# A graph layer with linear attention beside it: the attention's second half by tiles of nodes, turned for the projection two layers later

## The reference

```python
xn = layernorm(x)
# 1. four graph layers: gather the source rows, add the edge term, relu, sum at the target, two dense layers
for l in range(4):
    m = relu(h[src] + (edge_weight @ We[l] + be[l]))
    agg = segment_sum(m, dst)
    h = relu(relu(batchnorm(((1 + eps[l]) * h + agg) @ W1[l] + b1[l])) @ W2[l] + b2[l])
# 2. linear attention over the same xn, 8 heads of 64
q, k, v = fm(xn @ Wq + bq), fm(xn @ Wk + bk), xn @ Wv + bv      # fm(t) = elu(t) + 1
kv  = einsum('shd,she->hde', k, v)
z   = 1 / einsum('shd,hd->sh', q, k.sum(0))
att = einsum('shd,hde,sh->she', q, kv, z).reshape(s, 512) @ Wp + bp
x = x + h + att
# 3. a routed feed-forward block over layernorm(x), 8 experts, the best one for each node
```

## Time and profile before

| | |
|---|---|
| median of 3 runs | 1873.07 us |
| lowest and highest | 1863.77 and 1879.77 us |
| profiled execution, time | 1876.88 us |
| profiled execution, span | 1875.0 us |
| TensorE clock granted, mean | 0.934 of full |
| busy: TensorE, VectorE, ScalarE, GpSimd | 1551.8, 1280.2, 889.9, 1108.4 us |

### The profile page before, as it was taken

The page is one execution under the profiler, slowest core; times in us unless marked ns, Lnnn a source line. Parts: engine busy times, 40 slices in busy tenths (PEclk is TensorE's granted clock), DMA queues, the critical chain, the costliest instruction groups (busy, mean ns, idle before and its releaser), DMA issues.

```text
span 1875.0 us, 20514 instructions
## 1 busy us (share of the span) xinstructions
PE 1551.8 (83%) x6418; PEld 658.6 (35%) x6418; DVE 1280.2 (68%) x2344; ACT 889.9 (47%) x990; POOL 1108.4 (59%) x1073
## 2 busy tenths in 40 slices
PE   2677878766799888987899998997999989988694
PEld 2223333322343333332443333333433333334373
DVE  6678876768444999777546876876348877785533
ACT  1454443444305556665415665674146657663220
POOL 4777777777006767777016777774057777770122
PEclk8898999988999999999899998999999999998797
DMA  6767676667228867776238887874378887766244
GB/s 221 197 196 201 188 197 179 179 204 227 60 72 237 223 196 202 216 216 191 77 110 242 238 245 222 224 214 131 92 220 237 236 254 218 214 200 218 106 125 156
DMA packets 119349, 355.34 MB, mean 190 GB/s; under 512 B 19760, under 2 KB 24200, under 8 KB 118981
## 3 DMA queue, kind: packets, MB, share of 16 engines
q0 software_dynamic: 83600, 274.01, 51.6%
q1 hardware_dynamic: 35637, 79.95, 13.2%
HBM read 333.93 MB, written 19.95 MB: 189 GB/s over the span
## 4 chain that ended last, share of the span: by engine, by line
PE 46%; POOL 19%; DVE 12%; issue 9%; DMA 7%; ACT 7%; DVEq 0%; SPq 0%; POOLq 0%; ACTq 0%
PE ps L1523 42%; POOL ring L700 17%; DVE ring L876 6%; ACT ring L1350 6%; DMA ring<-x_table,idxT 4%; DMA zT<-slot_table 2%; PE ps L1588 2%; DVE xT L1086 1%; DVE aggT L1186 1%; POOL ring L743 1%; DMA mix<-in_edge_weight 1%; DVE lg L920 1%; ACT zT L1449 0%; PE ps L1929 0%; POOL ring L752 0%
## 5 line engine op out<-in xcount | busy, mean ns | idle before, releaser
L700 POOL DMA_INDIRECT ring<-x_table,idxT x1018 | 1063.2, 1044 | 582.0 <-issue 296.1
L876 DVE SCALAR_TENSOR_TENSOR ring<-we_bc,wT,ring 128x512 f32<-128x512 f32 x1018 | 689.8, 745 | 127.2 <-DMA ring<-x_table,idxT 127.0
L1350 ACT ACTIVATE ring<-ring 128x3072 f32<-128x3072 f32 (+1 forms) x165 | 446.8, 2709 | 372.1 <-DVE ring L876 371.9
L1523 PE MATMUL ps<-ring,onehot 128*32 128x512 f32 x2036 | 369.1, 659 | 205.6 <-ACT ring L1350 199.8
L1523 PE MATMUL ps<-ring,zT 126*128 126x512 f32 x720 | 336.5, 597 | 0.0
L1393 ACT ACTIVATE ring<-ps 128x512 f32<-128x512 f32 x228 | 128.2, 600 | 229.3 <-PE ps L1523 229.3
L920 DVE TENSOR_REDUCE lg<-ps 128x128 f32<-128x512 f32 x208 | 142.7, 686 | 114.4 <-PE ps L1588 59.3
L1523 PEld LDWEIGHTS ps<-ring,onehot 128*32 128x32 f32 x2036 | 73.0, 113 | 415.0 <-ACT ring L1350 266.7
L1523 PE MATMUL ps<-ring 128*32 128x512 f32 (+2 forms) x672 | 211.0, 543 | 5.6 <-DVE aggT L1186 5.6
L1523 PEld LDWEIGHTS ps<-ring,zT 126*128 126x128 f32 x720 | 126.3, 190 | 132.4 <-issue 112.3
L1523 PE MATMUL ps<-w,zT 128*125 128x512 f32 (+2 forms) x320 | 148.4, 627 | 22.1 <-ACT zT L1449 22.1
(11 more groups left out here) (252 smaller groups left out, 1202.9 us busy)
## 6 DMA issues: line engine op xcount, KB each, us to landing
zT<-slot_table SPq DMA_DIRECT2D x36, 625.0 KB
ring<-x_table,idxT POOLq DMA_INDIRECT x1018, 3.7
w<-in_L_gnn_W SPq DMA_DIRECT2D x8, 1024.0 KB, 11.4
ring<-in_L_ffn_W SPq DMA_DIRECT2D x16, 512.0 KB, 9.8
x_table<-ring SPq DMA_DIRECT2D x30, 250.0 KB
x_table<-ring SPq DMA_DIRECT2D x17, 256.0 KB
y_table<-aggT SPq DMA_DIRECT2D x17, 256.0 KB, 2.0
ring<-in_x SPq DMA_DIRECT2D x1, 2304.0 KB
```

What stands on the lines that cost most here:

```text
L700: gp.indirect_dma_start(out=slots[:, k, u, :], out_offset=None, in_=table[:, :], in_offset=bass.IndirectOffsetOnAxis(ap=idx, axis=0)).then ...
L876: ins = v.scalar_tensor_tensor(out=slots[:, k, u, :], in0=we_bc[:, :], scalar=wT[:, c, u:u + 1], in1=slots[:, k, u, :], op0=ALU.mult, op1= ...
L1350: a.activation(at, at, ACT.Relu).then_inc(relu_done, 1)
L1523: return nc.tensor.matmul(o, lhsT, rhs, start=start, stop=stop)
```

## The change

The att job is done by tile of 128 nodes, all 512 features in one: ten jobs instead of twelve, at j = 3, 4, ..., 15, 16. The query tile is now the stationary operand and `kvblk`, with the keys' sums of its two heads as two more columns (130 columns), the moving one: four matmuls into two banks. The result has nodes on partitions, so there is one denominator for each node and head: VectorE takes two reciprocals of 128x4 and multiplies two halves of 128x256, with the reciprocal broadcast. `ksblk` and `ksum` are gone, and the blocks job has one memset and eight copies with one wait at the end.

The projection needs the result as columns again. So in layers 2 and 3 a new job "columns" stands at j = 3, 6, ..., 15: four transposes on TensorE into `pick_fold`, and one copy of them into `mix` on ScalarE. "proj" moves to the step after it: j = 4, 7, ..., 16. SyncE's program is unchanged in its text.

```diff
-    ATT_AT = {3 * (i // 2 + 1) + i % 2: i for i in range(len(CUT) * KD)}
-    PROJ_AT = {2: {3 * (t + 1): t for t in range(NT // 2)}, 3: {3 * (t + 1): t + NT // 2 for t in range(NT - NT // 2)}}
+    ATT_AT = {3 * (t // 2 + 1) + t % 2: t for t in range(NT)}
+    COLUMNS_AT = {2: {3 * (t + 1): t for t in range(NT // 2)}, 3: {3 * (t + 1): t + NT // 2 for t in range(NT - NT // 2)}}
+    PROJ_AT = {l: {j + 1: t for j, t in at.items()} for l, at in COLUMNS_AT.items()}
...
+        def att_bank(b, r):
+            return (ps[6], ps[7])[b][0:r, 0:2 * (P + 2)].rearrange("p (a n) -> p a n", a=2)
...
-                    step(v.memset(kvblk[:, :], 0.0))
-                    step(v.memset(ksblk[:, :], 0.0))
+                    step(v.memset(kvblk[:, :, :], 0.0))
                     for b in range(2):
                         kvp = ps[6 + b][:, 0:2 * (P + 1)].rearrange("p (a e) -> p a e", e=P + 1)
-                        step(v.tensor_copy(ksum[:, 2 * b:2 * b + 2], kvp[:, :, P:].rearrange("p a e -> p (a e)")))
                         for h in range(2):
                             q = slice(h * HD, (h + 1) * HD)
-                            step(v.tensor_copy(by_tile(kvblk[q, :])[:, 2 * b:2 * b + 2, q], kvp[q, :, q]))
-                            for a in range(2 * b, 2 * b + 2):
-                                step(v.tensor_scalar(ksblk[q, a * P + h * HD:a * P + (h + 1) * HD], ones[q, 0:HD], ksum[q, a:a + 1], None, ALU.mult))
+                            v.tensor_copy(kvblk[q, 2 * b:2 * b + 2, q], kvp[q, :, q])
+                            ins = v.tensor_copy(kvblk[q, 2 * b:2 * b + 2, P + h:P + h + 1], kvp[q, :, P:])
+                    step(ins)
...
                 if kind == "att":
-                    step(v.reciprocal(att_inv(i, tiles), by_tile(den[:, 0:w])))
-                    v.tensor_tensor(mix[:, tiles[0]:tiles[-1] + 1, f * P:(f + 1) * P], by_tile(num[:, 0:w]), att_inv(i, tiles), ALU.mult).then_inc(att_ready, 1)
+                    for b in range(2):
+                        ins = v.reciprocal(sc[0:r, b, 0:KD].rearrange("p (a h) -> p a h", a=2), att_bank(b, r)[:, :, P:])
+                    step(ins)
+                    for b in range(2):
+                        ins = v.tensor_tensor(mix[0:r, i, b * 2 * P:(b + 1) * 2 * P].rearrange("p (a h e) -> p a h e", a=2, h=2),
+                                              att_bank(b, r)[:, :, 0:P].rearrange("p a (h e) -> p a h e", h=2),
+                                              sc[0:r, b, 0:KD].rearrange("p (a h) -> p a h", a=2).unsqueeze(3).to_broadcast([r, 2, 2, HD]), ALU.mult)
+                    ins.then_inc(att_ready, 1)
...
+                    if kind == "columns":
+                        a.wait_ge(att_turned, i + 1)
+                        a.activation(by_tile(mix[:, i, :])[:, :, 0:rows(i)], by_tile(pick_fold[:, :])[:, :, 0:rows(i)], ACT.Copy).then_inc(att_columns, 1)
...
-                    mm(by_tile(num[:, 0:w]), kvblk[:, f * P:(f + 1) * P], qT, True, True)
-                    mm(by_tile(den[:, 0:w]), ksblk[:, f * P:(f + 1) * P], qT, True, True).then_inc(nd_done, 1)
+                    for f in range(KD):
+                        ins = mm(att_bank(f // 2, r)[:, f % 2, :], mix[:, i, f * P:f * P + r], kvblk[:, f, :], True, True)
+                    ins.then_inc(nd_done, 1)
+                if kind == "columns":
+                    r = rows(i)
+                    if i > 0:
+                        pe.wait_ge(mix_done, i)
+                    picked_added(l, j)
+                    for c in range(KD):
+                        ins = pe.transpose(pick_fold[:, c * P:c * P + r], mix[0:r, i, c * P:(c + 1) * P], ident[0:r, 0:r])
+                    ins.then_inc(att_turned, 1)
                 if kind == "proj":
                     pe.wait_ge(wp_loaded, (l - 1) * 16)
-                    if i > 0:
-                        pe.wait_ge(mix_done, i)
-                    picked_added(l, j)
+                    pe.wait_ge(att_columns, i + 1)
```

More of the change, by code:

```diff
@@ L154, in beside_at @@
             return [("att", ATT_AT[j])]
+        if l > 1 and j in COLUMNS_AT[l]:
+            return [("columns", COLUMNS_AT[l][j])]
         if l > 1 and j in PROJ_AT[l]:
@@ L326, in build_gps_block @@
         b2g_bc = stage[:, 0, :]
-        kvblk = sb("kvblk", [P, D])
-        ksblk = sb("ksblk", [P, D])
-        k_bias = ksblk[0:1, :]
+        kvblk = sb("kvblk", [P, KD, P + 2])
+        k_bias = kvblk[0:1, :, :].rearrange("p k n -> p (k n)")[:, 0:D]
         parts = sb("parts", [P, 2, D])
@@ L361, in build_gps_block @@
         edge_sc = sb("edge_sc", [NC, 4])
-        ksum = sb("ksum", [P, KD])
         f_oh = onehot[:, SLOTS - 1, :, :]
@@ L469, in build_gps_block @@
         att_ready = sem("att_ready")
+        att_turned = sem("att_turned")
+        att_columns = sem("att_columns")
         proj_done = sem("proj_done")
@@ L520, in by_tile @@
             return ap.rearrange("p (t n) -> p t n", n=P)
-        def att_inv(i, tiles):
-            return xT[:, 0:len(tiles), 1024 + (i % 2) * P:1024 + (i % 2 + 1) * P]
         def early_bank(l, e):
@@ L548, in build_gps_block @@
         logit_bank = (ps[3], ps[0], ps[1])
-        nd_banks = (ps[6], ps[7])
+        def att_bank(b, r):
+            return (ps[6], ps[7])[b][0:r, 0:2 * (P + 2)].rearrange("p (a n) -> p a n", a=2)
         @block.sync
@@ L1077, in job @@
+                    step(ins)
                     v.sem_inc(kvblk_ready)
                 if kind == "att":
-                    tiles, f = TILES_OF_CUT[i // KD], i % KD
-                    num, den = nd_banks
-                    w = len(tiles) * P
+                    r = rows(i)
                     v.wait_ge(nd_done, i + 1)
-                    if i >= 2:
-                        v.wait_ge(att_ready, i - 1)
-                    step(v.reciprocal(att_inv(i, tiles), by_tile(den[:, 0:w])))
-                    v.tensor_tensor(mix[:, tiles[0]:tiles[-1] + 1, f * P:(f + 1) * P], by_tile(num[:, 0:w]), att_inv(i, tiles), ALU.mult).then_inc(att_ready, 1)
+                    for b in range(2):
+                        ins = v.reciprocal(sc[0:r, b, 0:KD].rearrange("p (a h) -> p a h", a=2), att_bank(b, r)[:, :, P:])
@@ L1452, in beside @@
             def beside(l, j):
-                for kind, i in act_jobs[j - 1] if l == 0 else []:
+                for kind, i in act_jobs[j - 1] if l == 0 else beside_at(l, j):
+                    if kind == "columns":
+                        a.wait_ge(att_turned, i + 1)
+                        a.activation(by_tile(mix[:, i, :])[:, :, 0:rows(i)], by_tile(pick_fold[:, :])[:, :, 0:rows(i)], ACT.Copy).then_inc(att_columns, 1)
                     if kind == "q":
@@ L1609, in early_sums @@
                     else:
-                        pe.wait_ge(att_ready, QS)
+                        pe.wait_ge(att_ready, NT)
                 if e % KD == 0:
@@ L1657, in fold_picked @@
                     pe.wait_ge(h_copied, early_before(l) + done)
-                done = [i for j in range(1, fold_step(q)) for kind, i in beside_at(l, j)]
+                done = [i for j in range(1, fold_step(q)) for kind, i in beside_at(l, j) if kind != "columns"]
                 if done:
@@ L1778, in job @@
                     picked_added(l, j)
-                    qT = mix[:, tiles[0]:tiles[-1] + 1, f * P:(f + 1) * P]
-                    mm(by_tile(num[:, 0:w]), kvblk[:, f * P:(f + 1) * P], qT, True, True)
-                    mm(by_tile(den[:, 0:w]), ksblk[:, f * P:(f + 1) * P], qT, True, True).then_inc(nd_done, 1)
+                    for f in range(KD):
+                        ins = mm(att_bank(f // 2, r)[:, f % 2, :], mix[:, i, f * P:f * P + r], kvblk[:, f, :], True, True)
+                    ins.then_inc(nd_done, 1)
+                if kind == "columns":
+                    r = rows(i)
+                    if i > 0:
[4 more added lines that the diff above has]
+                    ins.then_inc(att_turned, 1)
                 if kind == "proj":
```

## The result

The changed kernel takes 1939.19 us in the median of 4 runs (1934.16 to 1943.24), beside 1871.87 us for the kernel before (4 runs): a ratio of 1.0338, 95% interval 1.0304 to 1.0373. Forecast were 1911 us and a range of 1880 to 1930. The direction was right, the size was not: +67 us instead of +39. (In e5 to e15 the kernel before took 2099 to 2126 us, so of those only ratios within one comparison are used.)

The account below looks back on a forecast made before the run. VectorE was taken to bound the att jobs' steps in layer 1, TensorE the projections' steps. From the profiled 1876.9 us, -15 - 1.5 + 57.6 - 4.6 gave 1913.4, taken as 1911 us, range 1880 to 1930.

Parts of the forecast that it names:

- Layers 2 and 3: Steps with projections: slot lists issued later make each triple of steps longer; +28.8 us a layer, +57.6 for both.
- G + 8.85: Layers 2 and 3: SyncE issues the slot list 8.85 us after G, the group sums' start at j % 3 == 0.
- I take 12.0: Layers 2 and 3: a slot list's load takes 12.0 us from issue to use, bounds 10 and 14.
- List 8: Layers 2 and 3: slot list behind the second weights; its triple takes 36.4 us against 27.8, +8.6 a layer.
- Both layers, whose programs are the same: Layers 2 and 3: one layer's loss of +28.8 us taken for each, +57.6 together.
- Layer 1: Att jobs: eight full jobs' steps fall from 9.61 to 7.55 us, less 1.5 for slot lists; -15, range -17 to -8.
- Layer 0: Blocks job: eight spreading instructions, a memset and two copies leave VectorE, four small copies come; -1.5 us (0 to -3).
- The gathers' wait: Layer 3: a later chunk's 4.63 us wait for its gather goes, as gathers are further ahead; -4.6 us.
- The turn: Layers 2 and 3: four added transposes cost TensorE 0.65 us for each of ten jobs.
- B: Rival: lists come in time, load below 8.6 us, triples of layers 2 and 3 grow by 2.75; about 1883; chance 0.15.
- C: Rival: GpSimd's gathers, not the steps, set the end of layers 2 and 3; about 1858 us; chance 0.07.
- D: Rival: a list behind the x tile needs 14 us, or layer 1's att product isn't hidden; about 1930; chance 0.10.

Follow-up runs that it names:

- e5 to e15: Changed kernel unedited, with TensorE's wait filled, with all lists earlier, or with turn, projection and list 8 earlier; ratios to the kernel before 0.9948 to 1.0238.
- e1: Changed kernel with SyncE issuing slot lists 4 to 7 before its wait for the mix and the x tile load; 1902.98 us, ratio 1.0141.
- e2: Kernel before with only the projection moved one step later, no new attention and no turn; 1944.89 us, ratio 1.0363.
- e18: Changed kernel with every slot list issued before the wait for the mix, the eighth before the second weights too; 1881.47 us, ratio 1.0019.
- e17: Changed kernel with spare matmuls on TensorE before its wait for the relu in layers 2 and 3; 1932.31 us, ratio 1.0267.
- e16: Changed kernel unaltered, run again beside the kernel before, which took 1878.84 us; 1940.63 us, ratio 1.0323.
- e3: Changed kernel with the turn at j = 1, 4, ..., 13 and the projection back at j = 3, 6, ..., 15; 1866.24 us, ratio 0.9938.
- e4: Changed kernel without the turn, projection at its old steps on the unturned tile, so its product isn't the reference's; 1860.72 us, ratio 0.9917.

## Why the prediction was wrong in size

**Layers 2 and 3, forecast +57.6, measured +85.9** (steps 2 to 17, 42.1 + 43.8). The mechanism was right, as e1, e2 and e18 show. The step that failed is the list's issue at "G + 8.85". In the eight triples with lists 4 to 7 it comes at G + 11.0 in the mean (10.2 to 11.5), since the projection starts 5.5 us after G in the mean, behind group sums and a turn at 1.2 GHz, where the forecast had 3.2. Behind that start everything took what was forecast to 0.2 us, and in e17, where the clock was 1.00 and the filling didn't hold the sums up, the issue came at G + 8.8. The load, "I take 12.0", came out at 11.8 in the mean (9.4 to 14.0), and the way from L947 to the end of the next relu at 7.95, where the forecast had 8.03 to the sums. So a triple was 11.0 + 11.8 + 7.9 = 30.7 instead of 28.9. In the sum, eight issues 2.17 late are +17.4, the loads and the rest -3.

**List 8, forecast a triple of 36.4, measured 41.2 and 40.3:** together +8.7. Its group is first issued at G + 9.0 and G + 8.6 rather than G + 6.9, and takes 24.2 and 23.8 us to L947 instead of 21.5 to 22.3. The first part is the clock again, the second the load. In e16, the same kernel, these triples were 36.1 and 38.1, so this term is as uncertain as it is large.

**"Both layers, whose programs are the same."** The programs are, their times before were not: 123.8 us for these steps in layer 2, 117.7 in layer 3, where list 8 was waited for 3.6 us instead of 5.3 and the triple ahead of it took 22.8 instead of 25.1. Only layer 2's rows were read, so layer 3's loss came out 5.5 us too small. With the terms above: 57.6 + 17.4 - 3 + 8.7 + 5.5 = 86.2, against 85.9.

**Layer 1, forecast -15, measured -11.7.** VectorE's job shrank as said: of the 120 us of the window it is busy 100.28 instead of 112.44, in spite of more steps in it. The new reciprocals are as cheap as said, 0.17 us each; the line group of the window 595 to 750:

```profile
L1082 DVE RECIPROCAL sc<-ps 128x4 f32<-128x4 f32 x18 | 2.3, 167 | 2.5 <-PE ps L1527 2.5
```

Steps 2 to 17 take 118.6 us instead of 133.7, -15.1, as forecast; the steps before and behind them give 3.4 back. Not every step came down to 7.55 us, though: the third of each triple takes 8.5 to 9.2. And it is not a steady gain: the traces of e16, e17, e18, e1, e3 and e4, with the same program there, show -8.6, -10.3, -6.5, -4.4, -1.6 and -10.9. e2, with the old program, shows +1.7. The slot lists enter here too, by more than the 1.5 us that the forecast took off for them. A list was issued 15.0 us before its use in the kernel before and is issued 11.25 before it now, its buffer being freed by the takes; its load needs 11 to 14 us. In e18 two follow each other 28.7 us apart, where 23.6 is the pace of a list in time (VectorE's timeline):

```profile
624.05 0.89 DVE L948 TENSOR_SCALAR zT<-zT,node_up 125x1280 f32<-125x1280 f32 x1 [2.81 <-DMA zT<-slot_table]
652.77 0.89 DVE L948 TENSOR_SCALAR zT<-zT,node_up 125x1280 f32<-125x1280 f32 x1 [2.52 <-DMA zT<-slot_table]
```

That the load now sits at the edge in layer 1 is read from traces; no run tested it.

**Layer 0, forecast -1.5, measured -4.4:** the seven traces have -2.2 to -9.9 with one program, and e2, which has the old one, -6.2. So this is scatter, and no gain of the blocks job is shown. **The gathers' wait, forecast -4.6, all of it in layer 3:** steps 17 to 39 gave back 4.7, but 1.5 of them in layer 2, where VectorE's waits for gathers hardly changed (4.1 and 3.7 us). In layer 3 these waits fell from 6.4 to 2.0 us and the steps gave back 3.2. The sum fits better than its parts.

**The turn, 0.65 us each:** in e3 it costs its triple nothing. In the changed kernel's own place it shows no price either: e2, without it, loses as much in layers 2 and 3. **The last step of the sum:** 1913.4 less the 3.8 us of the profiled execution is 1909.6; the forecast took 1911, which changes nothing in the verdict.

**The rivals.** B, the lists in time, didn't happen, but e18 nearly made it happen: steps 2 to 17 of layers 2 and 3 then cost +13.5 and +16.4, 29.9 us together, where B had 29.6. That it fits so well is partly luck. The eight triples cost 27.6 us instead of 22, with the lower clock in six of them, and the two with list 8 cost 2.1 instead of 7.6. C, the gathers set the end, is out: the steps behind the jobs took back 4.7 of 86 us. D held the time (1925 to 1942), but not for its reason, a load of 14 us: the loads were 12 in the mean, and it was the issue that was late. The estimate of 3.5 us for a list, from the Trainium skill, page "DMA: Bandwidth & Descriptors", section "Anatomy of one DMA", is contradicted again: none of lists 4 to 8 in the changed kernel's layers 2 and 3 took less than 9.4. That section fits its figures to DMAs that GpSimd issues, and this load is SyncE's, a difference that the forecast didn't mention.

**The term that was missing.** That the new wait would lower the clock behind it stood in no term and in no rival, though the forecast put several microseconds of waiting ahead of TensorE. The rows of 0.50 behind waits of 6 to 8 us are the measured form of it. In the ten triples of the changed kernel TensorE waited 3.5 to 8.0 us, and the granted clock of the next 3.2 us was 0.50 to 0.59 in the mean. The Trainium skill, page "TensorE: Matmul & The Clock Gate", part 1, section "HAM oscillation", tells of a loop whose wait for a DMA in every round leaves the work behind it at 1.2 GHz each time; this case's rows agree, and a forecast that had drawn on it would have had the term.

## What to carry to other kernels

A step that is moved by one place takes with it whatever its semaphore releases on other queues: here one line of `PROJ_AT` cost 69 us, because SyncE's order tied a 12 us load to it, while the turn that made the move necessary has no price that can be told when it is put two steps ahead instead. When a wait is forecast for TensorE, look for a row behind a wait of that length and price the work behind it by that row, here 2.77 us in place of 1.48. Read every layer's own time before, not one for both. And where a load is the bound, try first to free it from the order it stands in: two moved lines in SyncE's program gave back 59 of 62 us.

## What the hardware showed that was not expected

- TensorE's level behind a short wait is not fixed by the wait alone: with 2.30 and 2.29 us idle before the sums, e18 shows a mean clock of 0.66 once and 1.00 the next time. The triple is 1.65 us longer for it.
- A load of 625 KB, lists 4 to 7 of layers 2 and 3, took from 9.4 to 14.0 us from issue to use in the changed kernel's trace, 9.5 to 14.3 in e16 (the same kernel) and 11.0 to 16.9 in e17.
- In e5 to e15 the kernel before took 12 to 13% longer, and the changed one lost less: 1.0175 and 1.0199 against 1.0338 and 1.0323. The mean granted clock of the kernel before was 0.89 to 0.91 there and 0.925 to 0.94 in e1 to e4 and e16 to e18; whether that is a cause or goes with another one stays open.
